# A graph network's edge stage: one load per attribute tile, its other 64 partitions filled by ScalarE copies

## The reference, cut to what matters

```python
# x (3125,128), src and dst (53125,) sorted by dst, edge_attr (53125,64)
for k in range(3):
    e = edge_vector @ edge_W[k] + edge_b[k]
    msg = relu(x[src] + e)
    agg = segment_sum(msg, dst, num_segments=n)
    z = (1 + eps[k]) * x + agg
    h = relu(batchnorm(z @ W1[k] + b1[k]))
    x = relu(layer_norm(h @ W2[k] + b2[k]))
return _layernorm(x_input + x)
```

## Time and profile before

| what | value |
|---|---|
| three executions, median | 1476.94 us |
| the profiled execution, own time | 1472.82 us |
| its span | 1470.9 us |
| PE busy over the span | 1256.8 us (85%) |
| DVE busy | 1041.0 us (71%) |
| ACT busy | 587.1 us (40%) |
| DMA traffic | 323.39 MB, mean 220 GB/s |
| granted TensorE clock, mean | 0.936 of full speed |

### The profile page before, as it was taken

The page is one execution under the profiler, slowest core; times in us unless marked ns, Lnnn a source line. Parts: engine busy times, 40 slices in busy tenths (PEclk is TensorE's granted clock), DMA queues, the critical chain, the costliest instruction groups (busy, mean ns, idle before and its releaser), DMA issues.

```text
span 1470.9 us, 37463 instructions
## 1 busy us (share of the span) xinstructions
PE 1256.8 (85%) x13834; PEld 1032.8 (70%) x13834; DVE 1041.0 (71%) x1871; ACT 587.1 (40%) x1157; POOL 896.0 (61%) x842
## 2 busy tenths in 40 slices
PE   2479889899888799889898589999998799999991
PEld 1245445454444688888888589999998689999991
DVE  7776667666877597778888666666666666667667
ACT  0234443443333144334444344444445244444451
POOL 0145556555565777656664277777773777777750
PEclk9699999999999799989999799999999899999995
DMA  7269889988888877666768657777778467777752
GB/s 169 68 219 278 266 282 275 275 282 271 283 250 281 255 232 212 204 203 199 240 195 261 182 155 233 220 214 237 218 222 246 136 208 221 213 226 215 222 160 67
DMA packets 261672, 323.39 MB, mean 220 GB/s; under 512 B 55303, under 2 KB 172089, under 8 KB 261537
## 3 DMA queue, kind: packets, MB, share of 16 engines
q1 hardware_dynamic: 208632, 218.82, 48.7%
q0 software_dynamic: 33280, 82.06, 17.2%
q10 hardware_dynamic: 19625, 20.58, 6.9%
HBM read 213.80 MB, written 107.55 MB: 218 GB/s over the span
## 4 chain that ended last, share of the span: by engine, by line
PE 31%; POOL 17%; DVE 15%; issue 15%; DMA 14%; ACT 3%; ACTq 3%; SPq 1%; DVEq 0%
POOL rows L601 16%; PE ps L1327 12%; DMA rows<-attr_dram 8%; PE ps L1356 4%; PE ps L1346 3%; DVE terms L951 3%; DMA relB<-relrow_dram 3%; PE ps L1297 2%; ACTq L385 2%; PE ps L1298 2%; PE ps L1299 2%; PE ps L1300 2%; PE ps L1301 2%; DVE hot_stage L978 1%; DMA rows<-table_dram,src_i 1%
## 5 line engine op out<-in xcount | busy, mean ns | idle before, releaser
L601 POOL DMA_INDIRECT rows<-table_dram,src_i x416 | 438.4, 1054 | 187.7 <-issue 181.6
L585 POOL DMA_INDIRECT srt_dram<-region,pos_i x208 | 240.1, 1154 | 241.7 <-ACT region L659 193.7
L601 POOL DMA_INDIRECT rows<-x_dram,src_i x208 | 215.4, 1035 | 98.8 <-issue 55.8
L1327 PE MATMUL ps<-xs,early_words 125*128 125x128 bf16 x2720 | 258.3, 224 | 15.9 <-issue 15.9
L1327 PE MATMUL ps<-xs,region 125*128 125x128 bf16 x2584 | 244.5, 224 | 17.7 <-issue 13.8
L1327 PE MATMUL ps<-xr,early_words 125*128 125x128 bf16 x1360 | 248.0, 224 | 0.0
L1327 PE MATMUL ps<-xr,region 125*128 125x128 bf16 x1292 | 234.8, 223 | 0.0
L1327 PEld LDWEIGHTS ps<-xs,early_words 125*128 125x128 fp8e4 x2720 | 222.7, 100 | 16.5 <-issue 16.4
L1327 PEld LDWEIGHTS ps<-xs,region 125*128 125x128 fp8e4 x2584 | 210.8, 100 | 18.2 <-issue 14.1
L1047 DVE TENSOR_TENSOR terms<-ps,terms 128x512 f32<-128x512 f32 x156 | 107.1, 687 | 157.6 <-PE ps L1327 152.1
L1297 PE MATMUL ps<-wf,rows 128*128 128x384 bf16 x416 | 142.1, 342 | 73.4 <-ACT region L655 53.8
(11 more groups left out here) (140 smaller groups left out, 2229.8 us busy)
## 6 DMA issues: line engine op xcount, KB each, us to landing
ep_dram<-terms SPq DMA_DIRECT2D x52, 768.0 KB, 5.4
terms<-srt_dram SPq DMA_DIRECT2D x156, 256.0 KB
terms<-ep_dram SPq DMA_DIRECT2D x156, 256.0 KB
early_words<-hotrow_dram SPq DMA_DIRECT2D x156, 104.0 KB
rows<-attr_dram SPq DMA_DIRECT2D x108, 128.0 KB, 4.2
rows<-attr_dram ACTq DMA_DIRECT2D x100, 128.0 KB
region<-kept_dram SPq DMA_DIRECT2D x13, 576.0 KB
early_words<-kept_dram SPq DMA_DIRECT2D x13, 576.0 KB
```

The costliest lines, as they stand in the source:

```text
L585: pool.indirect_dma_start(srt, bass.IndirectOffsetOnAxis(ap=pos_i[:, c:c + 1], axis=0), stage_s[:, q, t, :], None).then_inc(scattered[q], 16)
L601: pool.indirect_dma_start(rows[:, q, t * FEAT:(t + 1) * FEAT], None, source, bass.IndirectOffsetOnAxis(ap=src_i[:, c:c + 1], axis=0),).the ...
L1327: ins = nc.tensor.matmul(bank(q)[:, c:c + FEAT], hot_g[v % 2][0:SLICE, h, at:at + P], x_part(part, FIRST[t] + k), start=k == 0 and part == ...
```

## The change

`load_attr` issues one DMA instead of two and fills only partitions 0 to 63 of a slot. `split_attr` works on those 64 partitions. ACT writes both halves of the words in partitions 64 to 127: the second part from `attr_r` as before, now read from its partitions 0 to 63, and, behind a wait for DVE's L953 (`attr_low`), a copy of the third part from partitions 0 to 63. The counts in the waits follow. The lines of the new kernel differ by one or two: L644 stays, the new copy is L647, the old L655 is L657, the old L951 and L953 are L953 and L955.

```diff
@@ load_attr
-            for half in range(2):
-                eng.dma_start(attr_t[half * EDGE_FEAT:(half + 1) * EDGE_FEAT, slot, :],
-                              attr[b * EDGE_FEAT:(b + 1) * EDGE_FEAT, q * QUAD * P:(q + 1) * QUAD * P]
-                              ).then_inc(attr_loaded[slot], 16)
+            eng.dma_start(attr_t[0:EDGE_FEAT, slot, :],
+                          attr[b * EDGE_FEAT:(b + 1) * EDGE_FEAT, q * QUAD * P:(q + 1) * QUAD * P]
+                          ).then_inc(attr_loaded[slot], 16)
@@ second_part, ACT
-                    slot = 2 * kind + n % 2
-                    act.wait_ge(attr_rest, 2 * n + kind + 1)
-                    nc.scalar.activation(high(attr_t[EDGE_FEAT:P, slot, :], QUAD * P),
-                                         high(attr_r[EDGE_FEAT:P, kind, :], QUAD * P), ACT.Copy).then_inc(attr_mid, 1)
+                    slot, m = 2 * kind + n % 2, 2 * n + kind
+                    top, bottom = attr_t[0:EDGE_FEAT, slot, :], attr_t[EDGE_FEAT:P, slot, :]
+                    act.wait_ge(attr_rest, m + 1)
+                    nc.scalar.activation(high(bottom, QUAD * P), high(attr_r[0:EDGE_FEAT, kind, :], QUAD * P),
+                                         ACT.Copy).then_inc(attr_mid, 1)
+                    act.wait_ge(attr_low, m + 1)
+                    nc.scalar.activation(low(bottom, QUAD * P), low(top, QUAD * P), ACT.Copy).then_inc(attr_mid, 1)
@@ split_attr, DVE
-                    whole, left = attr_t[:, slot, :], attr_r[:, kind, :]
-                    dve.wait_ge(attr_loaded[slot], (n // 2 + 1) * 32)
+                    whole, left = attr_t[0:EDGE_FEAT, slot, :], attr_r[0:EDGE_FEAT, kind, :]
+                    dve.wait_ge(attr_loaded[slot], (n // 2 + 1) * 16)
                     if n >= 1:
-                        dve.wait_ge(attr_mid, m - 1)
+                        dve.wait_ge(attr_mid, 2 * m - 3)
@@ staged, PE
-                    pe.wait_ge(attr_mid, n * 2 + (kind + 1))
+                    pe.wait_ge(attr_mid, n * 4 + (2 * kind + 2))
```

More of the change, by code:

```diff
@@ L542, in _ @@
                 for slot in range(BLOCK_QUADS):
-                    sp.wait_ge(attr_loaded[slot], 32)
+                    sp.wait_ge(attr_loaded[slot], 16)
                 with sp.Fori(0, LAYERS) as l:
```

## The result

| what | before | after |
|---|---|---|
| median of 11 runs each | 1476.01 us | 1487.88 us |
| ratio, 95% interval | | 1.0075 (1.0055 to 1.0096) |
| profiled execution, own time | 1472.82 us | 1490.25 us |
| first weight load of the layers' scatter (start) | 496.1 us | 510.4 us |
| DMA traffic | 323.39 MB | 309.76 MB |

A forecast was written before the change was run, and what follows sets the result against it. Staging was taken as bound by a DVE path behind the comparisons, with 1.44 us a body open to faster loads. Copies +13.5 and loads -6 gave +7.5 us on 1476.9, so 1484.4; range 1466 to 1499.

The forecast's parts named there:

- its sign: Staging body, four steps: was to take 32.0 to 32.6 us in the changed trace, from 31.77 before.
- Closed path: Staging steps bound by DVE's comparisons: ScalarE's copies delay PE's restart by 1.04 us, 9.91 to 10.9.
- 13 paths: Staging paths where the copies count in full: 13 x 1.04 = +13.5 us.
- Price of the copy: Each ScalarE copy of 64 partitions by 512 elements: 0.78 us, ends 0.21 and 1.45.
- Loads: Single attribute load in the staging: slot full after 4.3 us on ACT's queue, 3.3 on SP's.
- down from 63 us to under half: Sign in the changed trace: the split's summed waits for attribute loads in the staging fall this far.
- Open steps: Two load-bound steps of each staging body: faster loads gain 0.6 us a body, 10 bodies, -6 us.
- the 1.44: Most that faster loads could win per staging body: 14.94 us for two steps PE could do in 13.50.
- Latency only: Rival: load landing is latency, not bytes, so only the second issue is saved; about 1497 us, chance 0.18.
- its second price: Latency rival's sum if 0.8 and not 0.5 us are saved per load: +17 us.
- The hidden copy: Rival: ScalarE's copies cost nothing and loads land early, 14.4 us less, about 1462 us; chance 0.14.
- No change: Rival: loads reach PE's pace in open steps, just paying for closed ones; sum -1, 1476 us, chance 0.18.

The follow-up runs named there:

- run 3: Changed kernel with DVE's two long comparisons of every fourth step moved ahead of the bias addition L963: 1456.95 us, ratio 0.9904 to the kernel before.
- run 4: Changed kernel with 18 unread PE matmuls at the start of each body's long gap, ScalarE waiting for them before its PSUM copy: 1482.21 us, ratio 1.0070.
- Runs 4 and 5: Changed kernel with 18 unread PE matmuls, in every body (1482.21 us, 1.0070), then only in bodies 3 to 12 (1805.81 us on a slower chip, 1.0008).
- run 1: Kernel before, keeping two loads and the 128-partition split, plus the changed kernel's ScalarE copies: 1497.11 us, ratio 1.016.
- run 2: Changed kernel with one load but without ScalarE's third-part copy, low half-words of partitions 64 to 127 left zero: 1466.96 us, ratio 0.9965.
- the kernel with both moves: Changed kernel, comparisons ahead of L963, ScalarE's PSUM copy and next load ahead of the second parts: 1782.62 us (0.9884) on the slower chip, 1432.49 (0.9717) on another.

## Why the prediction was right, and where its working was not

- **Direction and size.** Forecast +7.5 us on the median of the runs then shown, 1484.4; measured 1487.88, +11.9 on the medians and +0.75% in the ratio. The range held it. The body did not fit its sign: 33.27 us, where the forecast had 32.0 to 32.6.
- **Closed path**. The step is there, and run 3, which takes the comparisons off it, gains 1.7%. Its size was too large: PE's end before L963 (at 253.6) to the restart at 264.08 is 10.5 us, so +0.55 and not +1.04 (+0.51 in the mean of seven bodies). L953 to L657 grew by 0.70: activations one behind another start 0.64 to 0.80 us apart at 0.77 us of length, where my working set each behind the end of the last, and DVE's part came 0.13 earlier. Nor do 13 paths each add as much: the twelve such paths from the fourth step of the staging to its end add up to 126.6 us before and 130.1 after, +3.5 and not +13.5 (in the second profiles of both kernels, 129.7 and 129.6).
- **Price of the copy.** Right: 0.776 us in the mean against 0.78 taken, though it reads one half of the partitions and writes the other. DVE on 64 partitions (0.67 and 0.72 us against 0.69 and 0.75) cost as good as nothing, as taken.
- **Loads.** The direction was right and the size too small: 2.9 us in the median on SP's queue and 3.4 on ACT's, where I took 3.3 and 4.3; "down from 63 us to under half" is 16.2.
- **Open steps: the step that failed.** "Over the two open steps of a body I take -0.6 of the 1.44." They took 1.0 us more instead (14.84 to 15.86), though hardly a load is waited for. Where the clock stays up they do win: 13.84 us in run 4. What took the place of the wait is PE's clock: behind a gap of 3.7 to 3.9 us (by the starts) the matmuls run slow for 1.3 to 2.8 us of excess in each of the seven bodies. I had costed the clock at nothing and had it in no bound. Runs 4 and 5, which fill the gap, have such bodies two and three times in seven.
- **Rivals.** Latency only: refuted by the landing times (its second price should have read +18, 13.5 and 20 x 0.24, and not +17). The hidden copy: refuted by run 1 (+1.6%). No change: refuted by the ratio. Yet its mechanism is the one that the rows bear out but for the clock: loads reached PE's pace in the open steps and that paid for the closed ones, 31.27 us a body in run 4 without slow matmuls. The fall of the clock came on top.
- **The rules of the Trainium skill.** The Trainium skill says that a pair of loads to the two halves run behind one another ("SBUF — State Buffer", on issuing two DMAs to hit both halves). The runs fit it, as taking one away took more than half of the queue's engine time with it (17.7% to 6.4%), but none of them times one load of a pair against the other. By it the sum should have come out below the forecast; the measured one is above, by the clock. The Trainium skill's 2.0 us plus bytes over 436 GB/s ("DMA: Bandwidth & Descriptors", anatomy of one DMA) makes 2.3 us for 128 KB, as an estimate. The shortest loads land after 2.7 to 2.9 here. Its 0.3 us for the bytes saved does not carry over to queues in use, where SP's median fell from 4.3 to 2.9.

So the total was right by luck as much as by its working. At the end of the staging the profiles differ by 14.2 us (last product at 479.3 and 493.5): +3.5 on the closed paths, where I had +13.5, and +10.7 on all the rest, where I had -6. Two errors of opposite sign, 10 us on one side and 17 on the other, nearly cancelled, and most of the larger one is the clock that the sum left out (slow matmuls 10.7 us before, 24.9 after).

## What to carry to other kernels

When two bounds lie close to each other (here loads and a path that closes through another engine's in-order work), taking load off one of them buys little by itself: run 2 won 5 us, while load, comparisons and order together won 40 (1472.79 to 1432.49). Look at what stands in order ahead of the instruction that frees a resource: ScalarE was idle for 60% of the time from 100 to 400 us before the change, and still its copies cost 22 us; with the comparisons moved, putting the PSUM copy ahead of them won 26. A wait on PE can cost more than its own length, as its clock may fall behind it: put that into the sum, or at least into the upper bound, with the price that a row shows (here 1.6 us each time).

## What the runs showed of the hardware that I had not expected

- The length of the wait alone does not tell whether PE's clock falls behind it. Gaps of 3.7 to 3.9 us in the changed kernel were followed by slow matmuls in seven bodies of seven, in its second profile (3.3 to 3.8 us) in six of seven, one wait of 3.57 us being without. In run 2 waits of one length, 3.1 us, were followed by them in four bodies of seven. In the kernel before the waits of rows 8 (1.74 and 1.24 us) left the clock up, and four of 2.1 to 2.35 us did not, while two of 2.2 to 2.4 us did. All these are lengths by the starts but for those of rows 8. What decides stays open.
- On one chip the kernel before takes 1804 us where it takes 1473 to 1476 on others. Most of it is in the layers: for the same changed kernel the staging's last product came at 490 us there (493.5 on the other), and the layers took 1244 us (531.8 to 1775.4) instead of 940. But the kernel with both moves also had a body of 30.0 us in its staging there and of 27.7 on another chip, with 34.0 us of waiting and 13.0. Why stays open.
- An activation that reads 64 partitions and writes the other 64 took 0.776 us (L647; L644 in the changed kernel 0.762), one within its own half 0.779.
